# Weighted sums of four key tiles in a row, with eight buffers of probabilities, in a fused attention and FFN kernel

## The chip, the cores and the metric

The kernel runs on one core of a Trainium2 chip. The metric is the device time of one execution in microseconds. TensorE (PE in the profile) multiplies matrices, ScalarE (ACT) and VectorE (DVE) read its results from PSUM, GpSimd (POOL) works on SBUF alone, SyncE (SP) issues most DMAs.

## The reference

One pre-norm transformer block in float32: 2048 tokens of 128 channels, 16 heads of 64, then a gated FFN of 352 whose operands are quantised to FP4 in blocks of 16. Only the attention is touched by the change:

```python
qkv = x @ w_qkv
sim = jnp.einsum('bhid,bhjd->bhij', q, k) * scale
attn = jax.nn.softmax(sim, axis=-1)
out = jnp.einsum('bhij,bhjd->bhid', attn, v)
return out @ w_out + b_out
```

## The kernel before

**Units and steps.** The attention is cut into 32 units: 8 pairs of heads times 4 chunks of 512 queries. A unit has 16 steps (`j` = 0 to 15), one for each tile of 128 keys. Eight units make one pass of `body`, which runs four times (three in a hardware loop, the last one written out, with parts of the FFN quantisation placed inside its second half). Each engine has its own copy of this loop and they meet at semaphores only; on each engine the order is the order of the program.

**TensorE in one step.** `scores` makes the scores of the *next* key tile: three products (high and low parts of q and k), each for two heads, 64 rows x 128 columns of the array, into one of the two halves of `s_ps`. For the first two key tiles it adds the negated row maxima with two more matmuls (L964, 128 x 128), which wait for `spread`. `row_maxima` does one slot of the row maxima of a later unit: two matmuls (L971 and L978) into the two halves of `mx_ps`. It waits until ScalarE (`mx_rise`) and VectorE (`mx_free`) have both finished with the slot before, since `mx_ps` has no second buffer. At even `j` it stands ahead of `scores`, at odd `j` behind it. `misc` is one further product at some steps, given by `MISC_AT`: K at 1, raw at 3, the denominators (`den`) at 5, Q at 9, the output projection (`proj`) at 11, V at 13. All of them share the one bank `misc_ps`, and each waits on `misc_free` until the previous one has been read out. `weighted` adds probabilities times values of one key tile to `o_ps` (float32, 128 rows x 64 columns of the array, two heads; each takes two matmuls). In the kernel before, at every odd `j`, after all else, it does tiles `j - 1` and `j`.

**ScalarE in one step.** `probs[j % P_BUFS] = exp(scores)` (L569, 1024 columns), after `weighted` and the adds have released that buffer; then, at some steps, a copy out of `misc_ps` (`k_hi` at 2, `k_raw` at 4, `q_hi` at 10, `vv` at 14) or of `o_ps` (`copy_output` at 0); then `rises` (L496), the positive part of one half of `mx_ps`.

**VectorE in one step.** First `max_slot` (L741): it adds `rise` to the other half of `mx_ps` and takes the maximum. Behind it come, by step: at 1 `sum_tiles` (L782) and `k_low` (L728); at 5 the reciprocals (L759) of two quarters of the denominators, at 6 and 7 one quarter each, the last of which frees `misc_ps`; at 8 `normalise` (L767), on whose result `proj` waits; at 9 `q_low` (L732), which waits for ScalarE's `q_hi`; at 11 the addition of the projection; at 13 `neg_maximum`, with `spread` (L750); at 14 and 15 the last adds of probabilities.

**GpSimd** adds the probabilities of tiles 1 to 12 of a unit to `acc_pool` (L462), one add a tile. Its last sum is what `sum_tiles` takes up in the next unit.

Of the kernel before, what the change touches and what calls it, by code (L numbers as in the profile page):

```python
# [19 lines left out]
F32 = mybir.dt.float32  # L20
# [3 lines left out]
ACT = mybir.ActivationFunctionType  # L24
ALU = mybir.AluOpType
AX = mybir.AxisListType

P = 128
# [10 lines left out]
QC = 512  # L39
# [11 lines left out]
MAX_DONE = MAX_STEPS - AHEAD  # L51
SLOTS = 2 * ITEMS
LOWEST = -3.0e38
P_BUFS = 4
Q_BUFS = 4
POOL_TILES = 13
POOL_ADDS = POOL_TILES - 1
DVE_ADDS = STEPS - POOL_TILES - 1
K_AT, RAW_AT, DEN_AT, Q_AT, PROJ_AT, V_AT = 1, 3, 5, 9, 11, 13
MISC_AT = {K_AT: "K", RAW_AT: "raw", DEN_AT: "den", Q_AT: "Q", PROJ_AT: "proj", V_AT: "V"}  # L60
INVERT_AT = {DEN_AT: (0, 1), DEN_AT + 1: (2,), DEN_AT + 2: (3,)}
BACK = 2
START = 1
ZEROED = 2
WEIGHTS_AT = {6: {RAW_AT: "gate", V_AT: "up"}, 7: {RAW_AT: "down"}}
PRO_KQ = CHUNKS + 2
# [61 lines left out]
def misc_before(it, w, last):  # L128

    return it * (BODY * len(MISC_AT)) + sum(len(misc_at(v, last)) for v in range(w))  # L130
# [8 lines left out]
def block_kernel(nc, x_in, w_qkv, w_out, b_out, w_gate, w_up, w_down, out):  # L139
    ctx = ExitStack()  # L140
    with ctx:
        def sb(name, shape, dt=F32, stack=ctx):
            return stack.enter_context(nc.sbuf_tensor(name, shape, dt))

        def sem(name):
            return ctx.enter_context(nc.semaphore(name))
# [26 lines left out]
        attn = ExitStack()  # L173
# [12 lines left out]
        ones_r = sb("ones_r", [P, P], F32R, attn)  # L186
        probs = sb("probs", [P, P_BUFS, 2, QC], F32, attn)
        acc_pool = sb("acc_pool", [P, 2, 2, QC], F32, attn)
        acc_dve = sb("acc_dve", [P, 2, 2, QC], F32, attn)
        o_raw = sb("o_raw", [P, 2, QC], F32, attn)  # L190
        o_norm = sb("o_norm", [P, QC], F32, attn)
        rden = sb("rden", [P, QC], F32, attn)
        ones = sb("ones", [P, DH], F32, attn)
# [26 lines left out]
        o_ps = ctx.enter_context(nc.psum_tensor("o_ps", [P, QC], F32))  # L220
# [35 lines left out]
        pool_adds = sem("pool_adds")  # L256
        dve_adds = sem("dve_adds")
        den_acc = sem("den_acc")
        o_copied = sem("o_copied")
        o_normed = sem("o_normed")  # L260
# [31 lines left out]
        def at(it, per_unit, w, plus=0):  # L292

            return it * (BODY * per_unit) + (w * per_unit + plus)

        def after(it, per_unit, w, plus=0):

            return at(it, per_unit, w, plus) + START

        def par(w):  # L300

            return (w // CHUNKS) % 2

        def pool_free(it, w, j):

            t = j - P_BUFS
            if t >= 0:
                return pool_adds, after(it, POOL_ADDS, w, max(t, 1))
            t += STEPS
            if t < POOL_TILES:  # L310
                return pool_adds, after(it, POOL_ADDS, w, t - POOL_ADDS)
            return dve_adds, at(it, DVE_ADDS, w, max(t - POOL_TILES, 1))

        def ahead_of(w, j):
# [78 lines left out]
        def _(pool):  # L393
# [33 lines left out]
            pool.tensor_tensor(y[:, :, :], y[:, :, :], bias[:, :].unsqueeze(1).to_broadcast([P, N // P, DIM]),  # L427
                               ALU.add).then_inc(biased, 1)

            pool.sem_inc(pool_adds, START)  # L430

            def over_scale(n):
                src, _dst, width = quantised(n)
# [7 lines left out]
            def times_scale(n):  # L441
                kind, g = QUANTS[n]
                _src, dst, width = quantised(n)
                nb = width // BLOCK
                pool.wait_ge(f_grid, n + 1)
                if kind == "h" and g >= 2:
                    pool.wait_ge(f_ht, TQ * (g - 1))
                pool.tensor_tensor(by_block(dst), by_block(grid[buf(n)][:, 0:width]),
                                   each_block(bscale[:, n % 3, 0:nb], nb), ALU.mult).then_inc(f_quant, 1)

            def body(it, last):
                for w in range(BODY):
                    acc = acc_pool[:, w % 2, :, :]
                    for j in range(1, POOL_TILES):
                        if j == 1:

                            pool.wait_ge(den_acc, after(it, 1, w))
                        else:
                            pool.wait_ge(pool_adds, after(it, POOL_ADDS, w, j - 1))
                        pool.wait_ge(p_ready, after(it, STEPS, w, j + 1))  # L460
                        first = probs[:, 0, :, :] if j == 1 else acc
                        pool.tensor_tensor(acc, first, probs[:, j % P_BUFS, :, :], ALU.add) \  # L462
                            .then_inc(pool_adds, 1)
                        if last and w > CHUNKS and j == 9:
                            times_scale(w - CHUNKS - 1)
                    if last and w >= CHUNKS:
                        over_scale(w - CHUNKS)
# [11 lines left out]
        def _(act):  # L479
# [18 lines left out]
            def copy_output(it, w):  # L498

                act.wait_ge(pv_done, at(it, STEPS, w, P_BUFS))  # L500
                act.wait_ge(o_normed, after(it, 1, w))
                act.activation(o_raw[:, (w - 1) % 2, :], o_ps[:, :], ACT.Copy).then_inc(o_copied, 1)

            def split_weights(i, loaded):

                act.wait_ge(wqkv_loaded, loaded)
                act.activation(wqkv_hi[i][:, :, :], wqkv[:, :, :], ACT.Copy).then_inc(wqkv_high, 1)
# [25 lines left out]
            split_weights(1, 32)  # L533
            act.wait_ge(zeros_ready, ZEROED)
            act.sem_inc(p_ready, START)

# [25 lines left out]
            def body(it, last):  # L562
                for w in range(BODY):
                    for j in range(STEPS):
# [3 lines left out]
                        act.wait_ge(*pool_free(it, w, j))  # L568
                        act.activation(probs[:, j % P_BUFS, :, :], s_ps[:, j % 2, :, :], ACT.Exp, scale=SCALE) \  # L569
                            .then_inc(p_ready, 1)  # L570
# [62 lines left out]
        def _(dve):  # L633
# [129 lines left out]
            def normalise(it, w, last):  # L763

                dve.wait_ge(misc_free, misc_no(it, w, "den", last) + START + 1)
                dve.wait_ge(o_copied, at(it, 1, w, 1))
                dve.tensor_tensor(o_norm[:, :], o_raw[:, (w - 1) % 2, :], rden[:, :], ALU.mult).then_inc(o_normed, 1)  # L767

            def add_projection(it, w, last):

# [6 lines left out]
            def sum_tiles(it, w):  # L777

                sums = acc_dve[:, (w - 1) % 2, :, :]
                dve.wait_ge(pool_adds, after(it, POOL_ADDS, w))  # L780
                dve.wait_ge(dve_adds, at(it, DVE_ADDS, w, DVE_ADDS))
                dve.tensor_tensor(sums, sums, acc_pool[:, (w - 1) % 2, :, :], ALU.add).then_inc(den_acc, 1)  # L782

# [12 lines left out]
            for g in range(CHUNKS):  # L796
# [3 lines left out]
                    .then_inc(xt_split, 1)  # L800
            dve.sem_inc(den_acc, START)
            dve.sem_inc(o_normed, START + 1)
            dve.sem_inc(misc_free, START)
# [23 lines left out]
            def body(it, last):  # L827
                for w in range(BODY):
                    sums = acc_dve[:, w % 2, :, :]
                    for j in range(STEPS):  # L830
# [40 lines left out]
                        if j == POOL_TILES + 1:  # L871

                            dve.wait_ge(p_ready, after(it, STEPS, w, j + 1))
                            dve.tensor_tensor(sums, probs[:, (j - 1) % P_BUFS, :, :], probs[:, j % P_BUFS, :, :],
                                              ALU.add).then_inc(dve_adds, 1)
# [53 lines left out]
        def _(pe):  # L929
# [72 lines left out]
            for name, c in PRO_MM:  # L1002
# [31 lines left out]
                else:  # L1034
# [3 lines left out]
                    project(ps, 0, 0, c, xhat_hi, xhat_lo).then_inc(pro_mm, 1)  # L1038
            pe.wait_ge(zeros_ready, ZEROED)
            pe.wait_ge(pro_v, CHUNKS)  # L1040
# [46 lines left out]
            def weighted(it, w, j):  # L1087

                pe.wait_ge(p_ready, after(it, STEPS, w, j + 1))
                if j == 0:  # L1090
                    pe.wait_ge(o_copied, at(it, 1, w, 1))
                for h in range(2):
                    ins = pe.matmul(o_ps[DH * h:DH * (h + 1), :], vv[par(w)][:, j, DH * h:DH * (h + 1)],  # L1093
                                    probs[:, j % P_BUFS, h, :], start=(j == 0), stop=(j == STEPS - 1))
                ins.then_inc(pv_done, 1)
# [17 lines left out]
            def body(it, last):  # L1113
                for w in range(BODY):
                    ahead = not (last and w == BODY - 1)

                    pe.wait_ge(misc_free, misc_before(it, w, last) + START)
                    for j in range(STEPS):
                        if j % 2 == 0:
                            row_maxima(it, w, last, j)  # L1120
                        if j < STEPS - 1:
                            pe.wait_ge(p_ready, after(it, STEPS, w, j))
                            scores((j + 1) % 2, par(w), w % Q_BUFS, j + 1).then_inc(s_ready, 1)
                        elif ahead:
                            pe.wait_ge(p_ready, after(it, STEPS, w, j))
                            scores(0, par(w + 1), (w + 1) % Q_BUFS, 0, at(it, 1, w, 2)).then_inc(s_ready, 1)
                        if j % 2:
                            row_maxima(it, w, last, j)
                        if j in misc_at(w, last):
                            misc(misc_at(w, last)[j], it, w, last)  # L1130
                        if j % 2:

                            weighted(it, w, j - 1)
                            weighted(it, w, j)

            with pe.Fori(0, ITERS - 1) as it:
                body(it, False)
# [71 lines left out]
```

## Time and profile before

| | before |
|---|---|
| median of three runs | 1446.51 us (1444.43 to 1447.43) |
| the profiled execution's own time | 1444.27 us |
| its span, first to last instruction | 1442.4 us |
| PE busy | 1338.7 us, 93% |
| POOL busy | 1007.2 us, 70% |
| DVE busy | 980.2 us, 68% |
| ACT busy | 909.0 us, 63% |
| HBM traffic | 3 GB/s over the span |

The prologue lasts to about 83 us, the 32 units from there to about 1343 us, the rest is the FFN. DMA plays no part in the units. Busy shares are averages; which wait ends last is read from the order of instructions in time.

### The profile page before, as it was taken

Reading aid. Unit: us, or ns where it says so; the run is one execution under the profiler, and the core shown is the slowest. Engines: PE = TensorE matmul, PEld = TensorE weight load, DVE = VectorE, ACT = ScalarE, POOL = GpSimd, SP = SyncE. Lnnn points to the kernel's source line nnn. Section 1 sums busy time; section 2 is a strip of 40 time slices with the busy share of each in tenths; the row PEclk is TensorE's granted clock in tenths of the full one; section 3 lists DMA queues with packets and bytes.
Section 4 is the critical chain, followed back from the end, with each engine's and each line's share of the span. In section 5 each row is a group of like instructions: output and inputs, shape, how many; then the busy total and the mean of one; then the engine's idle time right before and its main releaser. Section 6 shows DMA issues by size and latency. Waiting matters only on the chain.

```text
span 1442.4 us, 24289 instructions
## 1 busy us (share of the span) xinstructions
PE 1338.7 (93%) x7541; PEld 688.9 (48%) x7541; DVE 980.2 (68%) x2216; ACT 909.0 (63%) x1292; POOL 1007.2 (70%) x423
## 2 busy tenths in 40 slices
PE   3699999999999999999999999999999999899576
PEld 2455445545454444544555455445455454443245
DVE  6356766677666776676666766676666667778794
ACT  3366666766666776666666667676667666564242
POOL 3067777777788777777677887777777779987332
PEclk9589999999999999999999999999999999999687
DMA  2000000000000000000000000000000000000001
GB/s 59 1 3 7 1 1 1 8 1 1 2 8 1 1 1 1 9 1 1 2 9 1 1 1 8 1 1 1 1 3 1 1 1 1 1 1 0 0 0 30
DMA packets 9074, 6.41 MB, mean 4 GB/s; under 512 B 480, under 2 KB 8800, under 8 KB 8944
## 3 DMA queue, kind: packets, MB, share of 16 engines
q1 hardware_dynamic: 8720, 4.26, 1.0%
q8 instruction: 66, 1.08, 0.3%
q0 software_dynamic: 224, 0.54, 0.1%
q14 instruction: 64, 0.52, 0.1%
HBM read 3.75 MB, written 1.05 MB: 3 GB/s over the span
## 4 chain that ended last, share of the span: by engine, by line
PE 67%; issue 17%; DVE 11%; ACT 2%; POOL 1%; DMA 0%; DVEq 0%; POOLq 0%; ACTq 0%; SPq 0%
PE o_ps L1093 26%; PE s_ps L958 18%; PE mx_ps L971 6%; PE mx_ps L978 4%; DVE acc_dve L782 3%; PE misc_ps L1083 2%; PE misc_ps L1075 2%; PE s_ps L964 1%; ACT rise L496 1%; PE misc_ps L933 1%; PE misc_ps L946 1%; DVE k_lo L728 1%; PE misc_ps L948 1%; PE misc_ps L947 1%; PE s_ps L1175 1%
## 5 line engine op out<-in xcount | busy, mean ns | idle before, releaser
L462 POOL TENSOR_TENSOR acc_pool<-acc_pool,probs 128x1024 f32<-128x1024 f32 x352 | 879.3, 2498 | 49.6 <-POOL acc_pool L462 36.8
L741 DVE CUSTOM_DVE_ANT_0 summed<-mx_ps,rise 128x512 bf16<-128x512 f32 x512 | 350.6, 685 | 342.4 <-issue 337.1
L569 ACT ACTIVATE probs<-s_ps 128x1024 f32<-128x1024 f32 x512 | 524.6, 1025 | 83.9 <-PE s_ps L958 29.3
L496 ACT ACTIVATE rise<-mx_ps 128x512 f32<-128x512 f32 x512 | 305.6, 597 | 335.0 <-PE mx_ps L978 280.5
L1093 PE MATMUL o_ps<-probs,vv 128*64 128x512 f32 x2048 | 497.1, 606 | 3.8 <-ACT probs L569 3.8
L462 POOL TENSOR_TENSOR acc_pool<-probs 128x1024 f32<-128x1024 f32 x32 | 77.1, 2410 | 283.5 <-ACT probs L569 283.5
L978 PE MATMUL mx_ps<-k_hi,q_hi 64*128 64x512 f32 x512 | 238.8, 466 | 25.4 <-DVE part_max L741 24.3
L971 PE MATMUL mx_ps<-k_raw,q_hi 64*128 64x512 f32 x512 | 239.7, 468 | 12.9 <-DVE part_max L741 8.5
L1093 PEld LDWEIGHTS o_ps<-probs,vv 128*64 128x64 f32 x2048 | 127.1, 136 | 224.0 <-issue 180.4
L958 PE MATMUL s_ps<-q_hi,k_hi 64*128 64x512 f32 x1024 | 208.1, 402 | 1.9 <-ACT probs L569 1.0
L958 PE MATMUL s_ps<-q_hi,k_lo 64*128 64x512 f32 x1024 | 202.8, 392 | 0.0
L958 PE MATMUL s_ps<-q_lo,k_hi 64*128 64x512 f32 x1024 | 202.3, 391 | 0.0
L971 PEld LDWEIGHTS mx_ps<-k_raw,q_hi 64*128 64x128 f32 x512 | 95.8, 187 | 218.4 <-issue 205.7
L759 DVE RECIPROCAL rden<-misc_ps 128x128 f32<-128x128 f32 x132 | 120.9, 938 | 11.6 <-PE misc_ps L1075 11.5
L978 PEld LDWEIGHTS mx_ps<-k_hi,q_hi 64*128 64x128 f32 x512 | 95.8, 187 | 63.1 <-issue 44.2
L958 PEld LDWEIGHTS s_ps<-q_hi,k_hi 64*128 64x128 f32 x1024 | 97.2, 186 | 32.8 <-issue 19.5
L958 PEld LDWEIGHTS s_ps<-q_hi,k_lo 64*128 64x128 f32 x1024 | 96.9, 185 | 22.6
L958 PEld LDWEIGHTS s_ps<-q_lo,k_hi 64*128 64x128 f32 x1024 | 97.1, 186 | 20.6
L750 DVE TENSOR_TENSOR spread<-ident,neg_max 128x1024 fp32r<-128x1024 f32 x32 | 94.5, 2954 | 1.1
L782 DVE TENSOR_TENSOR acc_dve<-acc_dve,acc_pool 128x1024 f32<-128x1024 f32 x33 | 91.8, 2781 | 0.2
L767 DVE TENSOR_TENSOR o_norm<-o_raw,rden 128x512 f32<-128x512 f32 x33 | 50.3, 1523 | 0.1
L964 PE MATMUL s_ps<-spread,ones_r 128*128 128x512 f32 x128 | 47.9, 457 | 2.1 <-DVE spread L750 2.1
(153 smaller groups left out, 1149.7 us busy)
## 6 DMA issues: line engine op xcount, KB each, us to landing
wqkv<-in_L_attn_w_qkv SPq DMA_DIRECT2D x8, 192.0 KB, 2.7
y<-in_L_attn_x SPq DMA_DIRECT2D x4, 256.0 KB, 4.4
out<-y SPq DMA_DIRECT2D x4, 256.0 KB, 2.3
wo<-in_L_attn_w_out SPq DMA_DIRECT2D x8, 64.0 KB, 1.9
wx<-in_L_ffn_w_down POOLq DMA_DIRECT2D x1, 176.0 KB, 5.6
wx<-in_L_ffn_w_gate POOLq DMA_DIRECT2D x1, 128.0 KB, 4.3
wx<-in_L_ffn_w_up POOLq DMA_DIRECT2D x1, 128.0 KB, 5.2
bias<-in_L_attn_b_out SPq DMA_DIRECT2D x1, 64.0 KB, 5.5
```

Source lines behind the costliest of these rows:

```text
L462: pool.tensor_tensor(acc, first, probs[:, j % P_BUFS, :, :], ALU.add) \
L496: act.activation(rise[:, bank, :], mx_ps[:, bank, :], ACT.Relu).then_inc(mx_rise, 1)
L569: act.activation(probs[:, j % P_BUFS, :, :], s_ps[:, j % 2, :, :], ACT.Exp, scale=SCALE) \
L741: dve.tensor_tensor_reduce(summed[:, :], mx_ps[:, h, :], rise[:, h, :], 1.0, LOWEST, ALU.add, ALU.max, part_max[:, slot:slot + 1]).then_in ...
L750: dve.tensor_tensor(spread[:, :, :].rearrange("p h (t q) -> p (h t) q", q=P), ident[:, :].unsqueeze(1).to_broadcast([P, 2 * TQ, P]), neg_m ...
L759: ins = dve.reciprocal(rden[:, cols], misc_ps[:, cols])
L782: dve.tensor_tensor(sums, sums, acc_pool[:, (w - 1) % 2, :, :], ALU.add).then_inc(den_acc, 1)
L958: ins = pe.matmul(s_ps[:, buf, h, :], stationary[rows, :], moving[rows, :], start=(n == 0 and j < BACK), stop=(n == 2 and j >= BACK), skip ...
L964: ins = pe.matmul(s_ps[:, buf, h, :], ones_r[:, :], spread[:, h, :], start=False, stop=True, skip_group_check=True)
L971: return pe.matmul(mx_ps[:, h, :], q_hi[q][rows, t * P:(t + 1) * P], k_raw[k][rows, g * QC:(g + 1) * QC], start=True, stop=True)
L978: return pe.matmul(mx_ps[:, h, :].rearrange("p (c n) -> p c n", n=HALF), q_hi[q][rows, t * P:(t + 1) * P], moving, start=True, stop=True)
L1093: ins = pe.matmul(o_ps[DH * h:DH * (h + 1), :], vv[par(w)][:, j, DH * h:DH * (h + 1)], probs[:, j % P_BUFS, h, :], start=(j == 0), stop=(j ...
```

## The change

`P_BUFS` goes from 4 to 8. `weighted` is called at `j` = 3, 7, 11 and 15 for four tiles each, and no longer at every odd `j` for two. `DEN_AT` goes from 5 to 7, and with it everything that is placed relative to it: the reciprocals from steps 5, 6, 7 to 7, 8, 9, `normalise` from step 8 to 10. `o_raw` has one buffer in place of two, and ScalarE waits for the normalisation of the unit before ahead of writing it. The semaphore of GpSimd's adds starts at 5 so that waits against its value stay positive. The places of K, raw, Q, proj and V, the order of `row_maxima` and `scores`, and all instructions themselves stay as they are.

```diff
-P_BUFS = 4
+P_BUFS = 8
+GROUP = 4
-K_AT, RAW_AT, DEN_AT, Q_AT, PROJ_AT, V_AT = 1, 3, 5, 9, 11, 13
+K_AT, RAW_AT, DEN_AT, Q_AT, PROJ_AT, V_AT = 1, 3, 7, 9, 11, 13
 MISC_AT = {K_AT: "K", RAW_AT: "raw", DEN_AT: "den", Q_AT: "Q", PROJ_AT: "proj", V_AT: "V"}
 INVERT_AT = {DEN_AT: (0, 1), DEN_AT + 1: (2,), DEN_AT + 2: (3,)}
...
+POOL_START = 5
...
-        o_raw = sb("o_raw", [P, 2, QC], F32, attn)
+        o_raw = sb("o_raw", [P, QC], F32, attn)
...
             def copy_output(it, w):
 
                 act.wait_ge(pv_done, at(it, STEPS, w, P_BUFS))
-                act.wait_ge(o_normed, after(it, 1, w))
-                act.activation(o_raw[:, (w - 1) % 2, :], o_ps[:, :], ACT.Copy).then_inc(o_copied, 1)
+                act.wait_ge(o_normed, after(it, 1, w, 1))
+                act.activation(o_raw[:, :], o_ps[:, :], ACT.Copy).then_inc(o_copied, 1)
...
                         if j in misc_at(w, last):
                             misc(misc_at(w, last)[j], it, w, last)
-                        if j % 2:
-
-                            weighted(it, w, j - 1)
-                            weighted(it, w, j)
+                        if j % GROUP == GROUP - 1:
+
+                            for i in range(j - GROUP + 1, j + 1):
+                                weighted(it, w, i)
```

## Rows read from the trace of the kernel before

**Rows 1.** The page, busy time: engine, us, share of the span, instructions.

```profile
PE 1338.7 (93%) x7541; PEld 688.9 (48%) x7541; DVE 980.2 (68%) x2216; ACT 909.0 (63%) x1292; POOL 1007.2 (70%) x423
```

**Rows 2.** PE timeline, steps 6 and 7: start, duration (us), line, operation, operands, count.

```profile
606.45 0.50 PE L971 MATMUL mx_ps<-k_raw,q_hi 64*128 64x512 f32 x1
...
606.79 0.39 PE L958 MATMUL s_ps<-q_hi,k_hi 64*128 64x512 f32 x2
...
608.18 0.39 PE L978 MATMUL mx_ps<-k_hi,q_hi 64*128 64x512 f32 x1
...
608.50 1.94 PE L1093 MATMUL o_ps<-probs,vv 128*64 128x512 f32 x8
610.36 0.50 PE L971 MATMUL mx_ps<-k_raw,q_hi 64*128 64x512 f32 x1
```

**Rows 3.** PE timeline, steps 0 to 3 of the same unit; brackets: idle before, releaser.

```profile
591.16 0.50 PE L971 MATMUL mx_ps<-k_raw,q_hi 64*128 64x512 f32 x1
...
593.76 0.39 PE L978 MATMUL mx_ps<-k_hi,q_hi 64*128 64x512 f32 x1
...
594.09 0.50 PE L933 MATMUL misc_ps<-dx_hi,wqkv_hi 128*128 128x512 f32 x1
...
594.98 1.94 PE L1093 MATMUL o_ps<-probs,vv 128*64 128x512 f32 x8
...
599.08 0.47 PE L978 MATMUL mx_ps<-k_hi,q_hi 64*128 64x512 f32 x1 [0.35 <-DVE part_max L741]
...
601.69 0.49 PE L971 MATMUL mx_ps<-k_raw,q_hi 64*128 64x512 f32 x1
```

**Rows 4.** DVE timeline, steps 1 and 2 of that unit.

```profile
594.21 0.69 DVE L741 CUSTOM_DVE_ANT_0 summed<-mx_ps,rise 128x512 bf16<-128x512 f32 x1 [1.80 <-issue]
...
594.82 2.89 DVE L782 TENSOR_TENSOR acc_dve<-acc_dve,acc_pool 128x1024 f32<-128x1024 f32 x1
597.63 0.68 DVE L728 TENSOR_TENSOR k_lo<-misc_ps,k_hi 128x512 fp32r<-128x512 f32 x1
598.24 0.68 DVE L741 CUSTOM_DVE_ANT_0 summed<-mx_ps,rise 128x512 bf16<-128x512 f32 x1
```

**Rows 5.** Waits of PE over the whole span: us in total, times, longest us.

```profile
PE mx_ps L978 <- DVE part_max L741: 24.3, 40, 4.3
```

**Rows 6.** The page, costliest groups: count, busy us, mean ns, idle before.

```profile
L462 POOL TENSOR_TENSOR acc_pool<-acc_pool,probs 128x1024 f32<-128x1024 f32 x352 | 879.3, 2498 | 49.6 <-POOL acc_pool L462 36.8
...
L759 DVE RECIPROCAL rden<-misc_ps 128x128 f32<-128x128 f32 x132 | 120.9, 938 | 11.6 <-PE misc_ps L1075 11.5
```

**Rows 7.** ACT timeline, step 10: the copy of Q.

```profile
614.00 0.61 ACT L490 ACTIVATE q_hi<-misc_ps 128x512 fp32r<-128x512 f32 x1
```

**Rows 8.** DVE timeline, step 9: the low part of Q behind it.

```profile
614.65 0.69 DVE L732 TENSOR_TENSOR q_lo<-misc_ps,q_hi 128x512 fp32r<-128x512 f32 x1 [0.81 <-ACT q_hi L490]
```

**Rows 9.** Lines L767, L750, whole span: count, ns min/median/max, first and last start.

```profile
L767 DVE TENSOR_TENSOR o_norm<-o_raw,rden x33: 692/1658/2183, 99.2 to 1355.6; 128x512 f32<-128x512 f32 x33
...
L750 DVE TENSOR_TENSOR spread<-ident,neg_max x32: 1226/3245/3410, 60.8 to 1300.1; 128x1024 fp32r<-128x1024 f32 x32
```

**Rows 10.** PE timeline, a late unit in which spread came late.

```profile
1257.35 0.74 PE L964 MATMUL s_ps<-spread,ones_r 128*128 128x512 f32 x2 [0.93 <-DVE spread L750]
```

**Rows 11.** PE timeline, first instruction of the next unit, after steps 12 to 15.

```profile
630.37 0.50 PE L971 MATMUL mx_ps<-k_raw,q_hi 64*128 64x512 f32 x1
```

**Rows 12.** PE timeline behind two edges of the hardware loop: step 0 each, later step 1.

```profile
394.71 0.47 PE L971 MATMUL mx_ps<-k_raw,q_hi 64*128 64x512 f32 x1 [1.49 <-issue]
...
711.07 0.47 PE L971 MATMUL mx_ps<-k_raw,q_hi 64*128 64x512 f32 x1 [1.88 <-issue]
...
716.34 1.94 PE L1093 MATMUL o_ps<-probs,vv 128*64 128x512 f32 x8
```

**Rows 13.** Stretch behind the second edge: us, busy of PE, PEld, DVE, ACT, POOL; then the granted clock.

```profile
713.00:717.00 4.00, 4.00 (x15) 2.24 (x17) 1.95 (x4) 2.99 (x4) 2.63 (x2) 0.61 0.00 0
```

More of the change, by code:

```diff
@@ L302, in par, with pool_after @@
             return (w // CHUNKS) % 2
+        def pool_after(it, w, plus=0):
+            return at(it, POOL_ADDS, w, plus) + POOL_START
         def pool_free(it, w, j):
@@ L307, in pool_free @@
             if t >= 0:
-                return pool_adds, after(it, POOL_ADDS, w, max(t, 1))
+                return pool_adds, pool_after(it, w, max(t, 1))
             t += STEPS
             if t < POOL_TILES:
-                return pool_adds, after(it, POOL_ADDS, w, t - POOL_ADDS)
+                return pool_adds, pool_after(it, w, t - POOL_ADDS)
             return dve_adds, at(it, DVE_ADDS, w, max(t - POOL_TILES, 1))
@@ L428, in _ @@
                                ALU.add).then_inc(biased, 1)
-            pool.sem_inc(pool_adds, START)
+            pool.sem_inc(pool_adds, POOL_START)
             def over_scale(n):
@@ L458, in body @@
                         else:
-                            pool.wait_ge(pool_adds, after(it, POOL_ADDS, w, j - 1))
+                            pool.wait_ge(pool_adds, pool_after(it, w, j - 1))
                         pool.wait_ge(p_ready, after(it, STEPS, w, j + 1))
@@ L766, in normalise @@
                 dve.wait_ge(o_copied, at(it, 1, w, 1))
-                dve.tensor_tensor(o_norm[:, :], o_raw[:, (w - 1) % 2, :], rden[:, :], ALU.mult).then_inc(o_normed, 1)
+                dve.tensor_tensor(o_norm[:, :], o_raw[:, :], rden[:, :], ALU.mult).then_inc(o_normed, 1)
             def add_projection(it, w, last):
@@ L779, in sum_tiles @@
                 sums = acc_dve[:, (w - 1) % 2, :, :]
-                dve.wait_ge(pool_adds, after(it, POOL_ADDS, w))
+                dve.wait_ge(pool_adds, pool_after(it, w))
                 dve.wait_ge(dve_adds, at(it, DVE_ADDS, w, DVE_ADDS))
```

## The prediction

> **What bounds the kernel now.** I read the page's busy line first: TensorE is busy 93% of the span, GpSimd 70%, VectorE 68%, ScalarE 63% [rows 1]. Then TensorE's timeline of one unit in the middle. Two plain steps last from 606.45 to 610.36, 3.91 us, with no idle time [rows 2]. So the kernel runs at TensorE's own pace, and what the other engines do in a step is hidden as long as it fits beside that. I then looked for the places where it hardly fits. In steps 0 to 3 the matmul of 599.08 waited 0.35 us for VectorE [rows 3], and such waits come 40 times, 24.3 us in all [rows 5]. They are the ends of one chain: a slot of row maxima (`row_maxima`) may start only when VectorE has read the slot before. The question is what this chain does when the weighted sums, which now stand between its links, are moved away.
>
> **Part 1, fewer changes of array shape (a gain).** In the plain pair the six pairs of score matmuls take 1.39 us, a slot of 0.23 us each [rows 2]. Around the weighted sums slots are longer: 0.34 from the first row-maximum slot to the scores, 0.32 from the last one to the weighted sums, and 1.86 for the eight float32 matmuls. Four pairs of these back to back I take at 0.43 us each, 1.72 us (the end of a group is 0.14 more; I have this split from the other rows' sums and it is an estimate: 3.91 - 8 x 0.23 = 2.07, of which 1.72 is work and 0.35 change of shape). One round trip into the 128x64 shape and out thus costs 0.34 us. The change halves them from eight to four a unit: -4 x 0.34 = -1.36 us. But K, Q and V (steps 1, 9, 13) now stand among 64x128 matmuls rather than beside weighted sums. Each has two edges of its own, 0.10 us each (0.34 less 0.23), where before it needed one more: +0.20 for each.
>
> The rule behind it is that of the Trainium skill, TensorEngine Tiling (Array Packing), section Key Properties: changing the tiling mode, not just the tile, drains TensorE. The trace agrees, at 0.34 us a round trip. By that rule alone the change gains, and it is the last rival below.
>
> **Part 2, what the chain costs without cover.** A slot at 593.76 is read by VectorE from 594.21 (0.45 later) [rows 3, 4]; the reading of 598.24 lasts 0.68 and the next slot starts at 599.08, 0.84 after its start. So two slots stand at least 0.45 + 0.84 = 1.29 us apart. The pattern of the steps is slot, scores; scores, slot; slot, scores; scores, slot. Between the slots of an odd step and the next even one nothing stood but the weighted sums and `misc`. Now there is only `misc`, and between steps 5 and 6 nothing. I go through the unit in quarters, times from the quarter's first slot.
>
> Steps 0 to 3. Before: 591.16 to 601.69, 10.53 us [rows 3]. VectorE at step 1 has `sum_tiles` (594.82, 2.89 us), `k_low` (597.63) and only then the slot of step 2 (598.24) [rows 4]. None of these depends on weighted sums or moves, so the slot of step 3 stays where it is, 7.92 us into the quarter. TensorE, without the weighted sums of 594.98, is there at about 5.6 (3.82 to the end of K, 0.34 + 1.39 for slot and scores) and idles 2.3 us. The 2.61 us from 599.08 to 601.69 stay, and two more tiles of weighted sums (1.72) come in behind. After: 7.92 + 2.61 + 1.72 = 12.25 us, **+1.72**.
>
> Steps 4 to 7. The slot of step 6 must be 1.29 behind that of step 5, where a slot of 0.23 would do: 1.06 us idle, and 0.10 for the restart. With one round trip less: +1.06 + 0.10 - 0.34 = **+0.82**. The denominators move from step 5 to 7, in the same shape as the weighted sums in both kernels: no cost on TensorE.
>
> Steps 8 to 11. Here the later denominators add waits. (a) Q needs `misc_ps`, which the last reciprocal frees; this one moves from step 7 to step 9, behind the reading of slot 9. Slot 9 starts at 0.34 + 1.39 = 1.73; its reading 0.45 later, 2.18; VectorE is on to the next after 0.61 (594.21 to 594.82) [rows 4], 2.79; the reciprocal takes 0.94 [rows 6], 3.73; 0.15 for the signal (598.24 + 0.69 to 599.08), 3.88. TensorE would be ready at 2.05: idle 1.83. (b) Q takes 0.89 as K does (594.09 to 594.98) [rows 3] and ends at 4.77, slot 11 could start at 6.50. But VectorE's `q_low` follows ScalarE's `q_hi` by 0.65 (614.00, 614.65) [rows 7, 8]; `q_hi` can start 0.45 after the last of Q's three matmuls started, 4.90, so `q_low` 5.55, the reading of slot 10 0.61 later, 6.16, slot 11 at 7.00: idle 0.50. (c) `normalise` now stands at step 10, from 6.77, for 1.66 us in the median [rows 9], to 8.43; `proj` can start at 8.58 rather than 7.42: idle 1.16. Sum 1.83 + 0.50 + 1.16 + 0.20 - 0.34 = **+3.35**. What queues behind the waiting Q on TensorE is everything up to the next weighted sums, so nothing absorbs it. (c) has bounds: `normalise` took 0.69 us at the least and 2.18 at the most, which moves the idle time between 0.19 and 1.68.
>
> Steps 12 to 15. V stands between slots 13 and 14; it streams as many columns as K, so at least 0.89 + 0.32, against 1.29: covered. `spread` is due at 4.56 + 0.80 = 5.36. Slot 13 is read from 2.18, `spread` starts some 0.4 after that reading's end, near 3.2. Its duration is 3.25 us as a median but 1.23 at the least [rows 9]. With 3.25 it ends at 6.5 and TensorE idles 1.2; such a wait has been seen [rows 10]. With 1.23 there is no wait. I take 1.23, since its long ones are those beside an add of GpSimd, and GpSimd's twelve adds (2.50 us each [rows 6], begun about 3 us into the unit) end some 35 us into a unit that lasts 45, about 3 us ahead of `spread` at 38: -0.34 + 0.20 = **-0.14**; the other end is +1.1.
>
> The skill says the same of the cause: SBUF — State Buffer, section Who interferes with whom, has a VectorE instruction with two SBUF inputs contend with a GpSimd instruction that reads SBUF. No run here shows yet that the time at step 13 is free of them.
>
> Sum: 1.72 + 0.82 + 3.35 - 0.14 = 5.75 us a unit, on 10.53 (591.16 to 601.69), 8.67 (to 610.36) and 20.01 (to 630.37), which is 39.21 [rows 2, 3, 11]. 32 units give **+184 us**. Units of the last pass lack K, raw, Q or V in part but have FFN steps on VectorE in their place; I give them the same. Prologue and FFN are untouched.
>
> **Part 3, the clock (a loss that depends on the waits).** Behind one edge of the hardware loop TensorE idled 1.88 us, and the granted clock of the stretch behind it was 0.61, so most of it at 1.2 GHz; behind another it idled 1.49 us and kept 2.4 GHz [rows 12, 13]. From the first slot to the weighted sums the slow one took 716.34 - 711.07 = 5.27 us against 3.82 [rows 3]: 1.45 us for one such event. The changed kernel has two idle times of about 2 us in each unit (2.3 and 1.83), 64 in all. With none followed by the slow clock this costs nothing, with all +93 us; between ends so far apart I take half, **+46 us**, as one of the two edges did it.
>
> **Parts at nothing.** Eight buffers only loosen waits; ScalarE's 909 us in all [rows 1] are at most 28 us of work in a unit of 45. In steps 4 to 7 the scores of step 7 need the exponential of step 6, which ends near 3.9, and TensorE gets there near 4.0: just hidden. One buffer for `o_raw`: `normalise` of step 10 is over long before the next unit's step 0; if it were not, the whole of ScalarE would queue behind it. The semaphore's start value costs nothing. Of DMAs none moves.
>
> **Sum.** 1444.3 + 184 + 46 = 1674 us. The profiled execution is 2.2 us under the median of the runs, which I leave aside.
>
> **The rivals.** (A) As forecast, 1600 to 1730: 0.80. The ends are no slow clock with the short `normalise` (184 - 0.97 x 32 = 153, so 1600) and two thirds of the events with a longer one (1730). (B) `spread` stays long, since GpSimd drags behind in the longer unit: +1.2 x 32 = 38 more, or ScalarE's queue cannot serve the burst (exp and rise one after the other, no overlap, with a copy between: up to 0.5 us a quarter, 64 us): 1710 to 1770, 0.07. For it speaks that ScalarE has almost no slack in steps 4 to 7. (C) A good part of the idle times closes, because the chain of slots runs shorter when VectorE is not disturbed, and the clock holds: 1460 to 1600, 0.08. Against it: the 1.29 and the 7.92 come from rows, not from a mean. (D) TensorE stays the bound and the fewer changes of shape are all that counts: -1.36 + 0.60 = -0.76 us a unit, -24 us, 1420: 0.04. It decides when the idle times of a unit sum to less than 0.76 us, and for that slots would have to follow each other without VectorE's reading between; the waits in [rows 5] speak against it. No measurable change: 0.01.
>
> About 0.2% (3 us) is what a measurement of this kernel can tell from none. Faster 0.04, same 0.01, slower 0.95. The range 1600 to 1730 is case A's own.
>
> **What will show it.** Each step has its mark: weighted sums x16 in one stretch of about 3.6 us; the slot of step 3 still 7.92 behind the unit's first, with over 2 us idle before it, released by VectorE's maximum; Q's first matmul released by the reciprocal (L759), 1.8 us idle; `proj` released by `normalise`; slot 6 1.3 behind slot 5; `spread` near 1.2 us; stretches of clock 0.5 behind the 2 us idle times. The forecast is wrong if TensorE's waits for VectorE stay near 24 us in total, or if units last under 43 us at the full clock.

## The result and the profile after

The changed kernel takes 1663.45 us (median of four runs, 1659.79 to 1671.51) against 1445.47 us of the kernel before: a ratio of 1.1525, with a 95% interval of 1.1498 to 1.1552. The forecast was 1674, in a range of 1600 to 1730. Span against span it is 1660.6 to 1442.4 us, 218.2 us more.

The page of the kernel after, busy time and TensorE's clock (line numbers are those of the new file, six higher here: L964 are the scores, L977 and L984 the row-maximum slots, L1099 the weighted sums):

```profile
PE 1387.7 (84%) x7541; PEld 735.0 (44%) x7541; DVE 935.4 (56%) x2216; ACT 897.9 (54%) x1292; POOL 1000.2 (60%) x423
...
PEclk8598999999999998999999989999999999999887
```

TensorE executes the same 7541 matmuls. It was busy 93% of the span [rows 1]; now it is busy 84%. Its idle time grew from 103.7 to 272.9 us, +169.2, and its busy time by 49.0. These two make the 218.2. So there are two losses: waits, and matmuls that take longer.

TensorE's waits in the kernel after, in total, times, longest:

```profile
PE mx_ps L984 <- DVE part_max L747: 83.2, 62, 2.2
PE misc_ps L939 <- DVE rden L765: 50.1, 30, 1.7
PE mx_ps L977 <- DVE part_max L747: 42.6, 45, 2.6
PE misc_ps L1089 <- DVE o_norm L773: 28.5, 30, 1.3
```

These are 204.4 us, all of them for VectorE, which itself is busy only 56%. In the kernel before, VectorE's maximum held TensorE up for 24.3 us at the line of [rows 5] and for 8.5 us at the other slot line, and neither the reciprocal nor the normalisation appeared. The growth, 171.6 us, is about the idle time gained, 169.2.

The timeline of TensorE through one unit at the full clock, with the quarters' first slots (691.58, 703.84, 713.31, 726.56, 736.58) and what waits in them (in brackets the idle time before the instruction, and what ended it):

```profile
691.58 0.49 PE L977 MATMUL mx_ps<-k_raw,q_hi 64*128 64x512 f32 x1
...
699.51 0.46 PE L984 MATMUL mx_ps<-k_hi,q_hi 64*128 64x512 f32 x1 [2.17 <-DVE part_max L747]
...
700.25 3.65 PE L1099 MATMUL o_ps<-probs,vv 128*64 128x512 f32 x16
703.84 0.50 PE L977 MATMUL mx_ps<-k_raw,q_hi 64*128 64x512 f32 x1
...
705.56 0.39 PE L977 MATMUL mx_ps<-k_raw,q_hi 64*128 64x512 f32 x1
706.84 0.46 PE L977 MATMUL mx_ps<-k_raw,q_hi 64*128 64x512 f32 x1 [0.89 <-DVE part_max L747]
...
713.31 0.50 PE L977 MATMUL mx_ps<-k_raw,q_hi 64*128 64x512 f32 x1
...
717.10 0.50 PE L939 MATMUL misc_ps<-xhat_hi,wqkv_hi 128*128 128x512 f32 x1 [1.67 <-DVE rden L765]
...
721.89 1.16 PE L1089 MATMUL misc_ps<-wo,o_norm 128*128 128x128 f32 x8 [1.18 <-DVE o_norm L773]
726.56 0.50 PE L977 MATMUL mx_ps<-k_raw,q_hi 64*128 64x512 f32 x1
...
736.58 0.49 PE L977 MATMUL mx_ps<-k_raw,q_hi 64*128 64x512 f32 x1
```

The unit lasts 45.00 us, its quarters 12.26, 9.47, 13.25 and 10.02, against 39.21 us before ([rows 2, 3, 11]). The slot of step 3 starts 699.51 - 691.58 = 7.93 us into the unit. Before it was 7.92 [rows 3]: VectorE's chain did not move, only TensorE's work was taken from in front of it and put behind.

Two units, the first without slow stretches and the second with two, from one normalisation to the next (us, busy and count of PE, PEld, DVE, ACT, POOL; clock):

```profile
674.85:719.97 45.12, 38.76 (x227) 20.36 (x227) 24.70 (x62) 26.45 (x38) 29.61 (x13) 1.00 0.02 7
624.91:674.85 49.94, 44.38 (x231) 22.53 (x229) 24.60 (x64) 26.73 (x38) 29.36 (x13) 0.88 0.00 1
```

The same work takes 5.6 us more of TensorE's time in the second one. Inside it, the matmuls right behind the long wait:

```profile
651.22 0.76 PE L984 MATMUL mx_ps<-k_hi,q_hi 64*128 64x512 f32 x1 [2.17 <-DVE part_max L747]
...
652.46 6.31 PE L1099 MATMUL o_ps<-probs,vv 128*64 128x512 f32 x16
```

The sixteen weighted matmuls took 6.31 us after this wait and 3.65 after the same one at 699.51. The granted clock is 0.50 from 651.0 to 657.8, so 1.2 GHz. Whether one such wait is followed by it differs from unit to unit. There are 28 slow stretches between 85 and 1560 us, at most two in a unit: 14 begin within 1.6 us of the end of the wait at slot 3, 10 behind Q's wait of 1.67 us, and 4 behind the wait of `proj` that follows Q's.

### The profile page after: what moved, and what is told of

The parts are those of the page before. It is cut to its first block, busy times and chain, and to the rows that moved or that the text cites. A ratio compares the mean times of both kernels' runs of the same rounds, so it can differ in the third digit from the quotient of the medians.

```text
span 1660.6 us, 24289 instructions
## 1 busy us (share of the span) xinstructions
PE 1387.7 (84%) x7541; PEld 735.0 (44%) x7541; DVE 935.4 (56%) x2216; ACT 897.9 (54%) x1292; POOL 1000.2 (60%) x423
## 3 DMA queue, kind: packets, MB, share of 16 engines
q1 hardware_dynamic: 8720, 4.26, 0.9%
q8 instruction: 66, 1.08, 0.3%
## 4 chain that ended last, share of the span: by engine, by line
PE 44%; issue 35%; DVE 15%; ACT 4%; POOL 0%; DMA 0%; DVEq 0%; ACTq 0%; POOLq 0%; SPq 0%
PE o_ps L1099 14%; PE s_ps L964 11%; PE mx_ps L977 3%; DVE rden L765 3%; DVE o_norm L773 3%; PE misc_ps L1089 3%; PE s_ps L970 2%; PE misc_ps L1081 2%; PE mx_ps L984 2%; ACT rise L502 1%; DVE k_lo L734 1%; PE misc_ps L952 1%; ACT probs L575 1%; ACT q_hi L496 1%; PE misc_ps L939 1%
## 5 line engine op out<-in xcount | busy, mean ns | idle before, releaser
L1099 PE MATMUL o_ps<-probs,vv 128*64 128x512 f32 x2048 | 506.5, 640 | 0.0
L984 PE MATMUL mx_ps<-k_hi,q_hi 64*128 64x512 f32 x512 | 243.0, 475 | 83.2 <-DVE part_max L747 83.2
L977 PE MATMUL mx_ps<-k_raw,q_hi 64*128 64x512 f32 x512 | 242.3, 473 | 44.7 <-DVE part_max L747 42.6
L1099 PEld LDWEIGHTS o_ps<-probs,vv 128*64 128x64 f32 x2048 | 148.1, 147 | 286.4 <-issue 265.9
L964 PE MATMUL s_ps<-q_hi,k_hi 64*128 64x512 f32 x1024 | 213.8, 405 | 2.2 <-ACT probs L575 1.5
L964 PE MATMUL s_ps<-q_hi,k_lo 64*128 64x512 f32 x1024 | 211.2, 400 | 0.0
L964 PE MATMUL s_ps<-q_lo,k_hi 64*128 64x512 f32 x1024 | 210.2, 398 | 0.0
L977 PEld LDWEIGHTS mx_ps<-k_raw,q_hi 64*128 64x128 f32 x512 | 97.3, 190 | 188.4 <-issue 115.9
L984 PEld LDWEIGHTS mx_ps<-k_hi,q_hi 64*128 64x128 f32 x512 | 97.3, 190 | 126.5 <-issue 107.5
L964 PEld LDWEIGHTS s_ps<-q_hi,k_hi 64*128 64x128 f32 x1024 | 101.6, 188 | 29.3 <-issue 16.1
L964 PEld LDWEIGHTS s_ps<-q_hi,k_lo 64*128 64x128 f32 x1024 | 102.9, 189 | 18.7
L964 PEld LDWEIGHTS s_ps<-q_lo,k_hi 64*128 64x128 f32 x1024 | 102.2, 188 | 16.8
L1089 PE MATMUL misc_ps<-wo,o_norm 128*128 128x128 f32 x264 | 45.2, 323 | 28.7 <-DVE o_norm L773 28.5
L939 PE MATMUL misc_ps<-xhat_hi,wqkv_hi 128*128 128x512 f32 x31 | 15.8, 508 | 50.2 <-DVE rden L765 50.1
L1089 PEld LDWEIGHTS misc_ps<-wo,o_norm 128*128 128x128 f32 x264 | 38.3, 223 | 42.6 <-DVE o_norm L773 35.1
```

What stands on the lines that cost most here:

```text
L964: ins = pe.matmul(s_ps[:, buf, h, :], stationary[rows, :], moving[rows, :], start=(n == 0 and j < BACK), stop=(n == 2 and j >= BACK), skip ...
L977: return pe.matmul(mx_ps[:, h, :], q_hi[q][rows, t * P:(t + 1) * P], k_raw[k][rows, g * QC:(g + 1) * QC], start=True, stop=True)
L984: return pe.matmul(mx_ps[:, h, :].rearrange("p (c n) -> p c n", n=HALF), q_hi[q][rows, t * P:(t + 1) * P], moving, start=True, stop=True)
L1089: ins = pe.matmul(ps[:, t * P:(t + 1) * P], o_norm[:, t * P:(t + 1) * P], wo[par(w - 1)][:, :], start=True, stop=True)
```

## The experiments

**Only the buffers.** GROUP back to 2 and DEN_AT to 5:

```diff
-GROUP = 4
+GROUP = 2
-K_AT, RAW_AT, DEN_AT, Q_AT, PROJ_AT, V_AT = 1, 3, 7, 9, 11, 13
+K_AT, RAW_AT, DEN_AT, Q_AT, PROJ_AT, V_AT = 1, 3, 5, 9, 11, 13
```

> The changed kernel with GROUP = 2 and DEN_AT = 5: only the eight buffers and the single o_raw are left of the change. Chain theory: no difference from the kernel before, 1441 to 1450 us. Rival, the single o_raw or the larger ring costs time: above 1460 us.

Measured 1444.22 us, ratio 0.9997 (0.9984 to 1.0009). Eight buffers and one `o_raw` are worth nothing, either way.

**Pairs, with late denominators.** Only GROUP back to 2:

```diff
-GROUP = 4
+GROUP = 2
```

> The changed kernel with GROUP = 2: weighted sums in pairs again, but eight buffers, late denominators (step 7) and one o_raw. Chain theory (the weighted sums hid VectorE's chain): the cover is back, and only Q's wait for the last reciprocal (1.8 us a unit) and proj's wait for the normalisation (about 0.8 us) stay, so units of about 41.8 us and 1530 to 1560 us in all. Rival, the late denominators cost nothing by themselves and grouping is the whole loss: 1446 us. Rival, eight buffers or the late denominators are the whole loss: 1663 us.

Measured 1545.3 us, ratio 1.0701 (1.0670 to 1.0732), in the range of the chain theory. TensorE's waits in this kernel:

```profile
PE misc_ps L939 <- DVE rden L765: 50.2, 30, 1.8
PE misc_ps L1089 <- DVE o_norm L773: 37.7, 26, 1.9
PE mx_ps L984 <- DVE part_max L747: 22.1, 40, 2.1
```

The slots wait no more than before (40 times, 22.1 us), and Q's wait for the last reciprocal is that of the changed kernel, 50.2 us in 30 units. The wait of `proj` came out at 1.5 us rather than 0.8, since the normalisation took 2.43 us in the median here. So the late denominators alone cost 101 us, nearly half of the loss: 88 us of it are these two waits, which are entirely new.

**Four in a row, with early denominators.** Only DEN_AT back to 5:

```diff
-K_AT, RAW_AT, DEN_AT, Q_AT, PROJ_AT, V_AT = 1, 3, 7, 9, 11, 13
+K_AT, RAW_AT, DEN_AT, Q_AT, PROJ_AT, V_AT = 1, 3, 5, 9, 11, 13
```

> The changed kernel with DEN_AT = 5: four tiles in a row, early denominators. Chain theory: the slot of step 3 stays 7.92 us into the unit; the denominators now stand between slots 5 and 6 and cover that gap, but the reciprocals behind them delay slot 7 by about 1 us; Q and proj no longer wait. Units of about 42.8 us where the clock holds, 1555 to 1600 us in all. Rival, the late denominators are the whole loss: 1446 us or below. Rival, ScalarE cannot serve the burst of exponentials: little changes, above 1630 us.

Measured 1593.09 us, ratio 1.1032 (1.1000 to 1.1064), at the upper end of the chain theory's range. Its timeline of TensorE:

```profile
755.25 0.47 PE L984 MATMUL mx_ps<-k_hi,q_hi 64*128 64x512 f32 x1 [2.16 <-DVE part_max L747]
...
756.00 5.35 PE L1099 MATMUL o_ps<-probs,vv 128*64 128x512 f32 x16
...
766.99 0.47 PE L984 MATMUL mx_ps<-k_hi,q_hi 64*128 64x512 f32 x1 [0.76 <-DVE part_max L747]
...
775.01 0.47 PE L977 MATMUL mx_ps<-k_raw,q_hi 64*128 64x512 f32 x1 [0.98 <-DVE part_max L747]
```

The wait before slot 3 is untouched, and the gap between slots 5 and 6 is covered by the denominators; slot 7 waits for the reading of slot 6 that now stands behind two reciprocals (0.76 us; 1 was expected). Slot 10 waits 0.98 us, which the expectation did not have: the reading of slot 9 stands behind the normalisation, now 2.07 us long. The weighted sums behind the long wait ran at the slow clock in this unit, and the unit lasts 44.4 us, as nearly all do here, 1.70 of it by the clock. The grouping alone costs 149 us with the denominators early, and the late denominators 101 without the grouping. Together they cost 218, which is 32 less than the sum. TensorE's waits for VectorE's maxima, reciprocals and normalisations grow by 111 us here, by 85 with the pairs and by 172 in the changed kernel, 24 less than the two together; the rest is in its busy time, where the slow clock shows.

**VectorE's long sum moved beside the weighted sums.** The changed kernel, with these steps of VectorE's order moved:

```diff
-                        if j == K_AT:
+                        if j == RAW_AT:
                             sum_tiles(it, w)
-                        if j == K_AT and not skipped("K", w, last):
+                        if j == K_AT + 1 and not skipped("K", w, last):
...
-                        if w % CHUNKS == 2 and j == 3 and not last:
+                        if w % CHUNKS == 2 and j == 11 and not last:
```

> The changed kernel with VectorE's sum_tiles at step 3 rather than 1, k_low at step 2 rather than 1, and the split of weights at step 11 rather than 3, so that VectorE's long sum lies beside the four tiles of weighted sums. Chain theory: TensorE's idle time before slot 3 (2.2 us) goes, the first quarter lasts 9.9 us instead of 12.3, units of 42.6 us at full clock, and there are fewer stretches at half clock: 1550 to 1590 us. Rival, the burst of exponentials or the grouping as such is the limit: 1630 us or more.

Measured 1532.43 us, ratio 1.0612 (1.0581 to 1.0643): 131 us off the changed kernel by moving what another engine does, and 18 us below the range expected. The first quarter in its timeline of TensorE:

```profile
795.03 0.50 PE L977 MATMUL mx_ps<-k_raw,q_hi 64*128 64x512 f32 x1
...
804.93 0.50 PE L977 MATMUL mx_ps<-k_raw,q_hi 64*128 64x512 f32 x1
```

It lasts 9.90 us, as expected (12.26 in the changed kernel, 10.53 before). More came from the third quarter, 12.39 us in this unit against 13.25: the normalisation took 1.04 us in the median rather than 1.86. The rest is the clock: 12 slow stretches in the 32 units, where the changed kernel has 28. That the normalisation is shorter because it meets GpSimd's adds at another moment is likely, but not shown. A burst of exponentials is not the limit: the burst is the same here.

**All four reciprocals beside the weighted sums.** The changed kernel, with one line:

```diff
-INVERT_AT = {DEN_AT: (0, 1), DEN_AT + 1: (2,), DEN_AT + 2: (3,)}
+INVERT_AT = {DEN_AT: (0, 1, 2, 3)}
```

> The changed kernel with all four reciprocals at step 7, beside the weighted sums. Chain theory: Q no longer waits (1.7 us a unit saved), but q_low then stands before slot 10's reading and the normalisation before proj, so some 0.5 to 1 us comes back: units of about 43.8 us at full clock, 1590 to 1620 us. Rival, each wait counts by itself: 1663 - 32 x 1.7 - its share of the slow clock = 1580 us or less.

Measured 1610.5 us, ratio 1.1153 (1.1125 to 1.1180), in the expected range, but not by the expected way. Q waits no more, and slot 11 waits 0.75 us for the reading behind `q_low`, in place of 0.32. The expected wait of `proj` did not come in the hardware loop, where the normalisation took only 0.69 us. So a unit at the full clock would last 42.6 us (45.00 - 1.67 - 1.18 + 0.43, or 44.30 - 1.70), not 43.8; the clock made up the difference. Its timeline of TensorE behind the wait at slot 3, and the stretch's clock:

```profile
840.88 0.47 PE L984 MATMUL mx_ps<-k_hi,q_hi 64*128 64x512 f32 x1 [2.16 <-DVE part_max L747]
...
841.64 5.35 PE L1099 MATMUL o_ps<-probs,vv 128*64 128x512 f32 x16
...
841.70:845.10 3.40, 3.40 (x10) 0.95 (x10) 0.43 (x2) 1.52 (x3) 3.08 (x3) 0.50 0.00 0
```

Here the slow stretch comes in every unit of the hardware loop, at nearly the same place of it: units of 44.30 us repeat, each with the clock at half for 3.40 us right behind this wait, at a price of 5.35 - 3.65 = 1.70 us. In the last pass `proj` waits 2.1 us again in four units, a second slow stretch stands behind that wait, and the units last 48 us.

**What a change of shape costs.** The kernel before, with its pair of weighted sums pulled apart:

```diff
                         if j % 2:
+                            weighted(it, w, j - 1)
                             row_maxima(it, w, last, j)
...
                         if j % 2:
 
-                            weighted(it, w, j - 1)
                             weighted(it, w, j)
```

> The kernel before with the pair of weighted sums pulled apart: the first of the two tiles ahead of the odd step's row-maximum slot and product, the second where both were. Eight round trips more between the 64x128 and the 128x64 shape in each unit, nothing else. If a round trip costs 0.34 us as read from the rows: +2.7 us a unit, +87 us, 1520 to 1540 us. Rival, the long slots around the weighted sums are not the change of shape: 1446 us.

Measured 1500.56 us, ratio 1.0391 (1.0366 to 1.0417): +56 us, clearly not nothing, but 31 less than the round trips alone and below the range expected. Its timeline of TensorE, two plain steps (6 and 7):

```profile
630.00 0.50 PE L971 MATMUL mx_ps<-k_raw,q_hi 64*128 64x512 f32 x1
...
634.26 0.49 PE L971 MATMUL mx_ps<-k_raw,q_hi 64*128 64x512 f32 x1
```

They last 4.26 us where they lasted 3.91 [rows 2], so a round trip costs 0.35 us and the prediction's 0.34 stands. Units grew by 2.02 us (41.20 against 39.18), not by eight times that. Most of the missing 0.8 us is in steps 2 and 3, which became shorter, 4.58 us against 4.84 (596.85 to 601.69 before): the tile now in front of slot 3 covers its wait. The rest is in steps 14 and 15, which grew by 0.14 us only.

**The waits taken away.** The changed kernel with DEN_AT = 5, the moves of the sum experiment, and

```diff
-INVERT_AT = {DEN_AT: (0, 1), DEN_AT + 1: (2,), DEN_AT + 2: (3,)}
+INVERT_AT = {DEN_AT + 1: (0, 1), DEN_AT + 2: (2, 3)}
...
-                        if j == DEN_AT + 3:
+                        if j == DEN_AT + 2:
                             normalise(it, w, last)
-                        if j == Q_AT and not skipped("Q", w, last):
+                        if j == Q_AT + 1 and not skipped("Q", w, last):
```

(the last two in VectorE's order).

> Four tiles in a row with the waits taken away: denominators at step 5, sum_tiles at step 3, k_low at 2, reciprocals two at step 6 and two at 7, normalise at 7, q_low at 10, the split of weights at 11. Chain theory: VectorE's long work lies beside the four tiles of weighted sums, and what is left is four round trips fewer against six extra edges (-0.8 us) and a wait of 0.5 us at slot 9: units of about 38.9 us and no stretches at half clock, 1425 to 1450 us, so at or just under the kernel before. Rival, the grouping as such costs (ScalarE cannot serve the burst, or the ring): 1480 us or more.

Measured 1433.32 us, ratio 0.9931 (0.9911 to 0.9951): faster than the kernel before, and 230 us faster than the changed one, with the same grouping on TensorE. Its timeline of TensorE, the first slots of four quarters in a row:

```profile
646.62 0.50 PE L977 MATMUL mx_ps<-k_raw,q_hi 64*128 64x512 f32 x1
...
656.66 0.50 PE L977 MATMUL mx_ps<-k_raw,q_hi 64*128 64x512 f32 x1
...
666.56 0.49 PE L977 MATMUL mx_ps<-k_raw,q_hi 64*128 64x512 f32 x1
...
675.23 0.50 PE L977 MATMUL mx_ps<-k_raw,q_hi 64*128 64x512 f32 x1
...
685.08 0.50 PE L977 MATMUL mx_ps<-k_raw,q_hi 64*128 64x512 f32 x1
```

10.04, 9.90, 8.67 and 9.85 us make 38.46, so 0.75 us less than 39.21, with no wait of TensorE for VectorE left inside the loop's units and the clock at 1.00 throughout it. The 0.75 looks like the prediction's 0.76 for the shapes, but it is another sum. From slot 2 to slot 3 it now takes 1.69 us, and before it took 2.23 (596.85 to 599.08):

```profile
660.54 0.46 PE L977 MATMUL mx_ps<-k_raw,q_hi 64*128 64x512 f32 x1
...
662.23 0.50 PE L984 MATMUL mx_ps<-k_hi,q_hi 64*128 64x512 f32 x1
```

The kernel before, the other end of that comparison ([rows 3] have 599.08):

```profile
596.85 0.50 PE L971 MATMUL mx_ps<-k_raw,q_hi 64*128 64x512 f32 x1
```

So 0.54 of the 0.75 is the wait of [rows 3], which is gone, and 0.21 is left for the shapes. By the prediction's prices these would be 0.42: three round trips fewer, not four, since the denominators at step 5 now stand alone, and six extra edges of 0.10. The expectation left out the old wait and the denominators' own round trip, and it had a wait of 0.5 us at slot 9 that did not come.

Over the first 24 units this kernel gains 20.6 us on the kernel before; 7.4 are lost again outside them (by the spans, 1429.2 against 1442.4 us). In the last pass `spread` is again long in four units, which last 39.2 to 39.6 us:

```profile
1078.60 0.73 PE L970 MATMUL s_ps<-spread,ones_r 128*128 128x512 f32 x2 [1.00 <-DVE spread L756]
```

Dearer is one unit behind them, 47.2 us against 39.2, in which VectorE also quantises weights of the FFN and TensorE waits five times, 0.9 to 2.2 us each. Why `spread` is long in that pass and not in the loop I did not try to find out.

## Why the prediction was right, point by point

**Quarter by quarter.** Forecast +1.72, +0.82, +3.35 and -0.14, in sum +5.75; measured +1.73 (12.26 against 10.53), +0.80 (9.47 against 8.67) and, for the second half, 23.27 against 20.01, +3.26 where +3.21 was forecast; in sum +5.79. Each step has its line above: slot 3 pinned by `sum_tiles`, slot 6 at 1.28 us behind slot 5, Q waiting for the reciprocal, `proj` for the normalisation. Inside the second half errors cancel: its three waits (1.67, 0.32 and 1.18) make 3.17 us where 3.49 was forecast, and the rest, given as a gain of 0.28 by the shapes, is a loss of 0.09. The normalisation took 1.86 us in the median, not 1.66.

**Spread.** I took the short end, 1.23 us. All 32 of the kernel after are (line L756: count, least, median and longest ns):

```profile
L756 DVE TENSOR_TENSOR spread<-ident,neg_max x32: 1224/1225/1227, 61.0 to 1520.0; 128x1024 fp32r<-128x1024 f32 x32
```

against a median of 3245 before [rows 9]. None of the 32 overlaps one of GpSimd's adds now, which paid back about 2 us of VectorE's time in each unit. The Trainium skill (SBUF — State Buffer, Who interferes with whom) has a VectorE instruction with two SBUF inputs contend with a GpSimd one that reads SBUF. The traces agree, and show who pays: whichever starts later. In the kernel before, an add of GpSimd starts just ahead of `spread`; in the kernel with the waits taken away one starts behind it:

```profile
623.24 2.35 POOL L462 TENSOR_TENSOR acc_pool<-acc_pool,probs 128x1024 f32<-128x1024 f32 x1 [0.16 <-POOL acc_pool L462]
623.35 3.32 DVE L750 TENSOR_TENSOR spread<-ident,neg_max 128x1024 fp32r<-128x1024 f32 x1
...
610.97 1.37 DVE L756 TENSOR_TENSOR spread<-ident,neg_max 128x1024 fp32r<-128x1024 f32 x1
611.41 3.18 POOL L468 TENSOR_TENSOR acc_pool<-acc_pool,probs 128x1024 f32<-128x1024 f32 x1 [0.16 <-POOL acc_pool L468]
```

All 29 long ones of the kernel before end 1.08 us behind the end of the add that was running when they started. In the kernel with the waits taken away, 25 adds began while `spread` was running: `spread` took 1.22 to 1.40 us, and those adds 3.2 to 3.4 us instead of 2.4.

**Shapes.** A round trip costs 0.35 us by the experiment with the pair pulled apart, 0.34 in the prediction. The 0.76 us a unit was not measured by itself: the last experiment has 0.21 for the shapes where the prediction's prices give 0.42, and the second half above misses the same way, though there part of it may be restarts behind waits (0.10 us each in steps 4 to 7, none given here). So the gain was probably put too high, by a few tenths of a us in a unit. The Trainium skill's rule on tiling modes (TensorEngine Tiling (Array Packing), Key Properties), that changing the mode drains TensorE, agrees with the 0.35 us. By that rule alone the forecast would have been 1420: the rival in which TensorE stays the bound failed because the weighted sums were also the cover of another engine's chain.

**The clock, mis-sized.** Forecast 46 us: 1.45 an event, in half of 64 waits. Over the first 24 units (from 109.11 to 1239.15 us, by the normalisations) a unit lasts 47.09 us in the mean where 45.00 is one at full clock, 2.1 us or 50 in 24 units. The kernel before lost 7 us over the same units against 24 plain ones of 39.18 (4.5 of them at two edges of the loop), so the growth is some 43 us, where the forecast has 35. The slow stretches were as many as forecast, 25 in these units against 24, but dearer. Twelve last 3.4 us and thirteen 6.8, and one of the long ones cost up to 2.7 us (6.31 against 3.65), where 1.45 was read from a single short one. The half was a choice between none and all, made from two edges of the loop; that about half of the waits were followed by a slow stretch is luck as much as reading.

**The last pass, the error the other way.** Its eight units were given the same +5.75 + 1.45 as the others, 58 us. Measured are 218.2 - 182.8 = 35 us outside the first 24 units (182.8 is 1130.04 against 947.28 us, the time from the first to the twenty-fifth normalisation in either kernel). Behind the twenty-fifth normalisation five units grew by 5.5 to 7.6 us, but the last three became shorter, by 2.1, 1.0 and 2.8 us. Some units of this pass lack K and Q, in some VectorE kept TensorE waiting already before (up to 4.3 us, [rows 5]), and no stretch was slow there after 1313 us. That some clock was too small and this too large is why the total lies only 11 us off; the two errors are no merit of the sum.

**The range.** Its lower end comes out of the terms named for it (1444.3 + 153 = 1597). The upper end does not: two thirds of the events are 62 us and the longest `normalise` adds 0.52 x 32 = 17, so 1707 and not 1730. The measured 1663.45 lies inside either.

**Parts at nothing.** Confirmed by the experiment with the buffers alone.

## What to carry to other kernels

Work on the busiest engine is also cover for what the others do in sequence. Before bunching or moving it, list the pairs of instructions between which it stood, and for each the chain on the other engines that runs meanwhile; a chain with a fixed place (here slot 3, 7.92 us into the unit) turns each microsecond taken from in front of it into idle time. Move the other engine's long pieces along with the cover: with the denominators at step 5, the same grouping costs 10% without that (1593.09 us) and gains 0.7% with it (1433.32). The changed kernel's 15% holds the late denominators too.

## What the runs showed of the hardware

Idle times of 2.2 us on TensorE were followed by the clock of 1.2 GHz in some units and not in others, at the same place of the program; in the changed kernel so were those of 1.67 us ahead of Q, 10 times. In two of the kernels the pattern settled: with all reciprocals at step 7 the slow stretch came once in each unit of the hardware loop, 3.40 us long, and the units repeated to 44.3 us; with early denominators they repeated to 44.4. So in these kernels idle times of about 2 us on TensorE cost not only themselves but, now and then or regularly, 1.7 to 2.7 us more behind them.

A change between the 64x128 and the 128x64 shape of the array and back cost 0.35 us (4.26 us against 3.91 for two plain steps).
